# Graph layer on one core: the message stage takes y rows from an on-chip table and sums equal sources before the second linear map

## The reference, cut to what matters

```
ys = xs @ w1_s * inv;  yv = einsum('nud,uv->nvd', xv, w1_v) * inv      # y, 256 per node
w  = radial network of edge_attr_8 (three linear maps)                 # wA, wB, wC, wD per edge
es, ev = ys[dst], yv[dst];  sh0, sh1 = edge_attr_4 split
m0a = wA * es * sh0;              m0b = wD * sum_d(ev * sh1) / sqrt(3)
m1a = wB * es * sh1 (per d);      m1b = wC * ev * sh0
ns = segment_sum([m0a, m0b], src);  nv = segment_sum([m1a, m1b], src)  # and the degree
out = ns * dn @ w2_s ...,  nv * dn @ w2_v ...                          # second linear map
```

## Time and profile before

| | us |
|---|---|
| runs, median of three (lowest to highest) | 8281.1 (8236.3 to 8301.24) |
| span of the profiled execution, first to last instruction | 7531.3 |
| median less that span | 749.8 |
| message stage in the profile, 2960 to 7237 | 4277, so 5.14 for each of 832 steps |
| attention stage, 170 to 2600 | 2430 |
| node stage, 2604 to 2955 | 351, so 3.58 for each of 98 blocks |
| last stage | 294 |

### The profile page before, as it was taken

One profiled execution on the slowest core, in us unless ns is written; L12 is line 12 of the kernel. 1 busy time (PEld: TensorE's weight loads), 2 busy tenths in 40 slices (PEclk: granted clock), 3 DMA queues, 4 the chain that ended last, 5 costly groups with the idle time before them and its releaser, 6 DMA issues.

```text
span 7531.3 us, 218435 instructions
## 1 busy us (share of the span) xinstructions
PE 6552.1 (87%) x36547; PEld 4301.1 (57%) x36548; DVE 5437.6 (72%) x20339; ACT 4022.4 (53%) x12733; POOL 5759.5 (76%) x4888
## 2 busy tenths in 40 slices
PE   6999999999999988888888888888888888888876
PEld 5666666666666555555555555555555555555544
DVE  3788888888888798666666666666666666666668
ACT  2455555555555455555555555555555555555532
POOL 3677777777777655888888888888888888888878
PEclk8899999999999999999999999999999999999999
DMA  5788888888888766777777777777777777777789
GB/s 178 200 224 223 224 225 224 222 224 226 224 223 223 207 221 192 136 136 135 136 135 135 136 136 136 136 135 136 135 135 137 136 136 135 136 136 135 136 227 299
DMA packets 1268411, 1312.20 MB, mean 174 GB/s; under 512 B 232303, under 2 KB 1153040, under 8 KB 1268272
## 3 DMA queue, kind: packets, MB, share of 16 engines
q0 software_dynamic: 368112, 577.39, 45.5%
q1 hardware_dynamic: 900258, 734.36, 33.8%
HBM read 723.28 MB, written 587.78 MB: 174 GB/s over the span
## 4 chain that ended last, share of the span: by engine, by line
PE 38%; issue 23%; POOL 19%; DMA 8%; DVE 7%; POOLq 2%; ACT 2%; DVEq 1%; ACTq 0%; SPq 0%
POOL part L571 13%; PE PS L845 12%; PE PS L837 12%; DMA part<-arena,c_idx 8%; POOL d_out L562 5%; PE PS L866 3%; PE PS L862 2%; PE PS L959 2%; PE PS L952 1%; PE PS L878 1%; ACT arena L724 1%; DVE arena L1310 1%; PE PS L871 1%; PE PS L789 1%; DVE arena L1298 1%
## 5 line engine op out<-in xcount | busy, mean ns | idle before, releaser
L571 POOL DMA_INDIRECT part<-arena,c_idx x1664 | 2671.4, 1605 | 515.8 <-issue 457.7
L522 POOL DMA_INDIRECT arena<-h_tab,sidx x1664 | 1773.8, 1066 | 634.9 <-issue 385.7
L1279 DVE SCALAR_TENSOR_TENSOR arena<-PS,c_src,lower_eq 128x128 f32<-128x128 f32 x1664 | 517.6, 348 | 1385.1 <-PE PS L964 1385.1
L717 ACT COPY arena<-PS 128x514 f32<-128x514 f32 x832 | 489.7, 589 | 1823.5 <-DMA part<-arena,c_idx 1823.3
L952 PE MATMUL PS<-ident,arena 128*128 128x128 f32 x3328 | 545.1, 286 | 679.7 <-ACT arena L724 666.5
L921 PEld LDWEIGHTS PS<-ident,arena 128*128 128x128 f32 x6656 | 739.8, 141 | 626.9 <-issue 582.7
L562 POOL DMA_INDIRECT d_out<-y_tab,c_row x832 | 829.2, 997 | 266.6 <-issue 252.6
L921 PE MATMUL PS<-ident,arena 128*128 128x128 f32 x6656 | 977.0, 280 | 61.5 <-issue 43.0
L710 ACT COPY arena<-PS 128x512 f32<-128x512 f32 x1664 | 991.7, 603 | 6.8 <-PE PS L921 6.7
L1157 DVE TENSOR_TENSOR big<-big,PS 128x260 f32 x1664 | 703.9, 423 | 396.2 <-PE PS L845 336.1
L845 PE MATMUL PS<-arena 128*128 128x260 f32 x3328 | 961.4, 412 | 3.5 <-DVE big L1157 2.2
(11 more groups left out here) (192 smaller groups left out, 11545.7 us busy)
## 6 DMA issues: line engine op xcount, KB each, us to landing
w_tab<-arena SPq DMA_DIRECT2D x416, 520.0 KB
arena<-w_tab SPq DMA_DIRECT2D x1664, 130.0 KB
part<-zeros SPq DMA_DIRECT2D x1664, 32.1 KB
arena<-part SPq DMA_DIRECT2D x392, 128.5 KB, 3.4
arena<-h_tab,sidx POOLq DMA_INDIRECT x1664
ot_tab<-arena SPq DMA_DIRECT2D x416, 64.0 KB
arena<-ot_tab SPq DMA_DIRECT2D x416, 64.0 KB
part<-arena,c_idx POOLq DMA_INDIRECT x1664
```

The costliest lines, as they stand in the source:

```text
L522: pool.indirect_dma_start(hg[:, s, k, :], None, h_tab, bass.IndirectOffsetOnAxis(ap=sidx[:, s, k:k + 1], axis=0)).then_inc(s_hg[s], 16)
L571: pool.indirect_dma_start(part[q], bass.IndirectOffsetOnAxis(ap=c_idx[:, s, k:k + 1], axis=0), o_cmb[:, q, :], None, compute_op=ALU.add).t ...
```

## The change

1. The node stage splits each y into three bfloat16 parts that add up to it, kept on chip in `y3` (ACT writes the high and the middle part, DVE makes the two remainders). y_tab, its stores and the gathers are gone; both tiles of every pair get y rows by PE, as the sum of three bfloat16 products for each tile. ot_tab now holds all four one-hot matrices of a group. Its bfloat16 form is used as it is.
2. `same` is now the plain equality of sources, without `lower_eq` and counts. The messages are multiplied by it where they were transposed (`combine`, L915): that product is the transposed sum over equal sources, so the product after the second map and one evacuation are gone.
3. Four small PE products for each pair (`count`) give the degree and a number that tells which edge of a source is its first; ACT copies them to `c_num`, DVE compares for the row numbers.
4. The numbers of blocks for y are loaded eight at a time, once in four steps, on PE.
5. Buffers move: the attention stage's lie beside `acc` in `big`, `o_cmb` has four slots, `midT` one instead of two.

```
 node stage, ACT and DVE
-                    a.copy(acc[:, ds(b - 2, 1), 0:D]..., maps[:, :, 0, :]).then_inc(s_bout, 1)
+                    a.copy(y3[:, ds(b - 2, 1), 0, :]..., maps[:, :, 0, :])
+                if there(b - 2):
+                    wait(act, s_br, b - 1)
+                    a.copy(y3[:, ds(b - 2, 1), 1, :].rearrange("p o d -> p (o d)"), b_r[:, s % 2, :]).then_inc(s_bmid, 1)
+                if there(b - 3):
+                    wait(dve, s_bmid, b - 2)
+                    v.tensor_tensor(y3[:, ds(b - 3, 1), 2, :]..., b_r[:, (s + 1) % 2, :], y3[:, ds(b - 3, 1), 1, :]..., ALU.subtract).then_inc(s_blo, 1)
+                if there(b - 2):
+                    wait(dve, s_bout, b - 1)
+                    v.tensor_tensor(b_r[:, s % 2, :]..., maps[:, :, 0, :], y3[:, ds(b - 2, 1), 0, :]..., ALU.subtract).then_inc(s_br, 1)
 message stage, POOL
-                n = (s + 6) % TURN
-                if n % 2 and there(u + 6):
-                    wait_apart(pool, s_crow, u + 7)
-                    wait_apart(pool, s_cmid, u + 3)
-                    for k in range(PAIR):
-                        pool.indirect_dma_start(c_y[:, n // 2, k, :], None, y_tab, ...)
-                    wait_apart(pool, s_cix, 3 * (u + 1))
+                    wait_apart(pool, s_cix, 2 * (u + 1))
-                                                o_cmb[:, q, :], None, compute_op=ALU.add).then_inc(s_add[q], 16)
+                                                o_cmb[:, s, k, :], None, compute_op=ALU.add).then_inc(s_add[q], 16)
 message stage, PE
-                def transpose(k):
+                def combine(k):
                     wait(pe, s_cmid, u)
                     wait(pe, s_cmT, PAIR * (u - 2) + k + 1)
                     for j in range(4):
-                        last = nc.tensor.transpose(PS[:, T_BANK[k], j * P:(j + 1) * P], mid[...], ident[:, :])
+                        last = mm(PS[:, T_BANK[k], j * P:(j + 1) * P], mid[...], same[:, m, k, :], start=True, stop=True)
                     last.then_inc(s_cmt, 1)
+                def count():
+                    wait(pe, s_cnum, u - 1)
+                    for k in range(PAIR):
+                        eq = same[:, m, k, :].bitcast(BF16)[:, 1::2]
+                        mm(counts[:, k, 0:1], eq, valid[:, ds((u - 1) * PAIR + k, 1)], start=True, stop=True)
+                        last = mm(counts[:, k, 1:2], eq, rank_b[:, :], start=True, stop=True)
+                    last.then_inc(s_ccnt, 1)
-                if n % 2 == 0 and there(u + 1):
-                    b = numbers(pe, block_row, (u + 1) * PAIR, PAIR, NB)
+                if s == 0 and there(u + 1):
+                    turn_blocks[0] = numbers(pe, block_row, (u + 1) * PAIR, (TURN if there(u + 4) else TURN - 1) * PAIR, NB)
-                    wait(pe, s_cotf, u + 3)
                     wait(pe, s_cmid, u)
+                    b = turn_blocks[0][s * PAIR:(s + 1) * PAIR]
                     for k in range(PAIR):
-                        last = mm(PS[:, 0, k * D:(k + 1) * D], c_otf[:, n // 2, k, :], acc[...], start=True, stop=True)
-                    last.then_inc(s_cy, 2)
+                        for i in (2, 1, 0):
+                            last = mm(PS[:, Y_BANK[n % 2], k * D:(k + 1) * D], c_ot[:, n // 2, n % 2 * PAIR + k, :],
+                                      y3[:, ds(b[k], 1), i, :]..., start=(i == 2), stop=(i == 0))
+                    last.then_inc(s_cy, 1)
-                if there(u - 3):
-                    wait(pe, s_csame, PAIR * (u - 2))
-                    wait(pe, s_cosb, u - 2)
-                    wait(pe, s_ccmb, u - 3)
-                    for k in range(PAIR):
-                        last = mm(PS[:, 6 + k, 0:OR], same[:, o, k, :], o_sb[:, o % 2, k, :], start=True, stop=True)
-                    last.then_inc(s_cc, 1)
 message stage, ACT (the whole of a step now)
+                if there(u - 2):
+                    wait(act, s_ccnt, u - 1)
+                    a.copy(c_num[:, (s + 2) % TURN, :, :], counts).then_inc(s_cnum, 1)
+                if there(u - 3):
+                    wait(act, s_co, u - 2)
+                    for k in range(PAIR):
+                        wait(act, s_add[q + k], 8 * (u - 3) - 8 * (o % 2) - 16 if there(u - 7) else 0)
+                    a.copy(o_cmb[:, o, :, 0:D]..., PS[:, O_BANK, :]...)
+                    a.copy(o_cmb[:, o, :, D], c_num[:, o, :, 0]).then_inc(s_ccmb, 1)
                 if there(u - 2):
                     wait(act, s_coT, u - 1)
                     a.copy(oT_sb[:, :, :], PS[:, OT_BANK, :]...).then_inc(s_coTsb, 1)
                 if there(u - 1):
                     transposed(0)
                     transposed(1)
```

More of the change, by code:

```diff
@@ new lines, in bass_gat_equivariant_kernel, with cut_of @@
+        big = sb("big", [P, BIG])
+        ACC = BIG - NB * HW
+        TABLES = 2 * EW + 2 * T + 4 * NC * P
+        assert ACC * NB >= 0 and TABLES <= NB * HW and (3 * D // 2 - HW) * NB <= ACC
+        acc = big[:, ACC:].rearrange("p (b d) -> p b d", d=HW)
+        y3 = big[:, :].bitcast(BF16).rearrange("p (b i d) -> p b i d", i=3, d=D)
+        tables = big[:, ACC:]
+        ARENA = 10400
+        arena = sb("arena", [P, ARENA])
+        used = {}
+        def cut_of(name, where, limit, n, at=None):
+            at = used.get(name, 0) if at is None else at
+            used[name] = at + n
+            assert used[name] <= limit, (name, used[name], limit)
+            return where[:, at:at + n]
@@ new lines, in bass_gat_equivariant_kernel @@
+        bounds = cut_a(2)
+        cnt = cut_a(8)
+        two = cut_a(33)
+        b128 = cut_a(NC)
+        tile_col = cut_a(NC)
+        wcol = cut_a(NC).bitcast(I32)
+        skw = cut(2 * D, True).rearrange("p (k n) -> p k n", k=2)
+        brow = cut(D)[0:1, :]
+        wm = cut(4 * P).rearrange("p (k m u) -> p k m u", k=2, m=2)
+        ones = cut(P)
+        pself = cut(NB * H).rearrange("p (b h) -> p b h", h=H)
+        rden = cut(NB * H).rearrange("p (b h) -> p b h", h=H)
+        B_KEPT = used["arena"]
@@ L718, in step_c @@
-                if there(u + 1):
-                    wait_apart(act, s_cix, 3 * (u - 2))
-                    a.copy(c_src[:, n, :], srcF[:, ds((u + 1) * PAIR, PAIR)]).then_inc(s_csl, 1)
+                    a.copy(midT[:, k, :, :], PS[:, T_BANK[k], :].rearrange("p (c e) -> p c e", c=4)).then_inc(s_cmT, 1)
+                if there(u - 2):
+                    wait(act, s_ccnt, u - 1)
+                    wait(act, s_cix, 2 * (u - 5))
+                    a.copy(c_num[:, (s + 2) % TURN, :, :], counts).then_inc(s_cnum, 1)
@@ L937, in step_c @@
                 if there(u - 1):
-                    transpose(0)
-                if n % 2 == 0 and there(u + 1):
-                    wait(pe, s_cotf, u + 3)
+                    combine(0)
+                if there(u + 1):
+                    if n % 2 == 0:
+                        wait(pe, s_cin[n], landed(u + 1, n, 2))
                     wait(pe, s_cmid, u)
+                    b = turn_blocks[0][s * PAIR:(s + 1) * PAIR]
                     for k in range(PAIR):
-                        last = mm(PS[:, 0, k * D:(k + 1) * D], c_otf[:, n // 2, k, :],
-                                  acc[:, ds(b[k], 1), 0:D].rearrange("p o d -> p (o d)"), start=True, stop=True)
-                    last.then_inc(s_cy, 2)
+                        for i in (2, 1, 0):
+                            last = mm(PS[:, Y_BANK[n % 2], k * D:(k + 1) * D], c_ot[:, n // 2, n % 2 * PAIR + k, :],
+                                      y3[:, ds(b[k], 1), i, :].rearrange("p o d -> p (o d)"),
+                                      start=(i == 2), stop=(i == 0))
+                    last.then_inc(s_cy, 1)
@@ L946, in step_c @@
                 if there(u - 1):
-                    transpose(1)
+                    combine(1)
+                    count()
                 if there(u - 2):
                     wait(pe, s_coTsb, u - 1)
-                    wait(pe, s_cosb, u - 2)
+                    wait(pe, s_ccmb, u - 2)
                     for j in range(4):
-                        last = nc.tensor.transpose(PS[:, 5, j * P:(j + 1) * P], oT_sb[:, j, :], ident[:, :])
+                        last = nc.tensor.transpose(PS[:, O_BANK, j * P:(j + 1) * P], oT_sb[:, j, :], ident[:, :])
@@ L966, in _ @@
-            steps(pe, NU, 1, 3, step_c)
+                    wait(pe, s_csame, u + 1)
+                    mm(PS[:, SR_BANK, 0:PAIR * P], ones_b[:, :], c_parts[:, n // 2, n % 2 * PAIR * P:(n % 2 + 1) * PAIR * P],
+                       start=True, stop=True).then_inc(s_csr, 1)
+            steps(pe, NU, 1, 2, step_c)
             pe.wait_ge(s_ccmb, NU)
@@ L1255, in step_b @@
                     wait(dve, s_brstd, b)
-                    wait(dve, s_bst[m], landed(b - 5, m, 2) if there(b - 5) else 0)
+                    wait(dve, s_bst[m], landed(b - 5, m) if there(b - 5) else 0)
                     normalized(b_x1[:, m, 0:MUL], b_v[:, m, 0:MUL], m).then_inc(s_bx1, 1)
```

(6 more changed lines are left out.)

352 lines of the change are left out of this document (152 added, 200 removed).

## The result

| | us | runs |
|---|---|---|
| before, median (lowest to highest) | 8258.7 (8225.79 to 8301.24) | 4 |
| changed kernel | 8973.53 (8937.48 to 8992.4) | 4 |
| ratio, 95% interval | 1.0868 (1.0823 to 1.0913) | |

The forecast was 8305 us with a range of 8020 to 8560 us. The time lies 413 us above the range.

What follows compares the result with a forecast made beforehand. POOL's queue was taken as the bound, PE close behind. Changed, PE's 4.54 + 0.55 us made a 5.10 us step; span 7531.3 - 34 + 65 - 7 = 7555, plus 749.8 around it: 8305 us, range 8020 to 8560.

Steps and rivals of the forecast that it cites:

- POOL bounds the kernel before: Message stage: POOL's scatters and gathers set the 5.11 us step; without gathers its queue falls to 3.81 us.
- PE's step: Message stage: PE's own work sums to 4.54 us a step, before the wait for block numbers.
- Combining: PE, message stage: 16 instructions of combining products at the transposes' 0.117 us each, 1.87 us a step.
- The switches: PE, message stage: four more changes of product form, 0 to 0.4 us a step, taken as 0.1.
- Rival (b): PE, message stage: weight loads of 128-column float32 products aren't hidden; at 0.14 us a load 8613 us; chance 0.15.
- Rival (c): PE, message stage: combining products cost four times the transposes seen, 0.47 us each; 9861 us; chance 0.02.
- The loop through ACT: Message stage: with one midT the second map waits for ACT's copy; a 4.45 us floor hidden under PE's 4.54.
- Node stage: Two added DVE subtractions of 256 columns, 0.66 us a block: 65 us more, range 25 to 95.
- Attention stage: PE's work there is unchanged and ot_tab's stores double: 0, at most 20 us more.
- The block numbers: PE, message stage: loading eight takes 3.16 us; PE stands 2.0 to 2.2 us once in four steps, taken as 0.55 a step.
- a rival on the fast side: Message stage: numbers load in 0.33 us, starting early, and switches cost nothing; 4.75 us a step, 8004 us; chance 0.27.
- 749.8 us around the span: Outside the traced span: 749.8 us of unexplained time, left unchanged and added to the 7555 us span.

Runs made afterwards that it cites:

- between_transposes: As load_behind, but load of two numbers ahead of the counts, and eight transposes instead of the combining products (sum over equal sources left out): 6479.78 us, third chip.
- load_behind: Changed kernel, with PE loading two block numbers every step, behind both sets of combining products and the counts: 7055.9 us, 0.9384 of the kernel before, second chip.
- shifted_numbers: Changed kernel with the row of block numbers shifted six places, so loads of eight start at multiples of 32 bytes: 7655.85 us, 1.0185 of the kernel before, second chip.
- two_numbers: Changed kernel, with PE loading two block numbers in every step at the same place, instead of eight once in four: 7988.9 us, 0.9675 of the kernel before.

## Why the prediction was wrong

Right, by the prediction's own steps:
- **POOL bounds the kernel before, and its queue falls to 3.81 us a step.** Met at 3.78 us once PE was made short enough (between_transposes).
- **PE's step.** 4.54 us forecast; 4.48 in the undisturbed step shown, 4.45 in the mean without numbers. Combining 1.87 us forecast, 1.89 measured (5003.53 to 5005.42 in load_behind); y 0.65 forecast, 0.66 measured (5006.23 to 5006.89). The switches were misread, with little effect: rows 6 leave 0.62 less 0.43, 0.19 us, for one change of form, not 0.1. Rival (b) falls: a weight load lasts 0.192 us and still hides. Rival (c) falls: by it the step would be 6.97 us. The Trainium skill, "TensorE: Matmul & The Clock Gate", Terms, says that the transpose mode is four times as fast for FP32. Measured against a float32 product, it is twice as fast here (0.109 against 2 x 0.112 us), and the measurement decides.
- **The loop through ACT.** Forecast as a floor at 4.45 that costs nothing; the second map waited for ACT 5 times in the stage, 1.9 us in all (the changed kernel on the third chip). That the step without numbers is 4.45 us too is no proof of the floor.
- **Node stage.** 65 us more forecast; L1242 starts 98 times from 3296.5 to 3703.8 us, 4.20 us a block, where it was 3.54 (L1249, 3229.6 to 3573.5, in the same chip's run of before): 0.66 us, 64 us. Its rows: 

```profile
L1242 DVE TENSOR_TENSOR arena<-arena,PS x98: 405/408/422, 3296.5 to 3703.8; 128x256 f32<-128x256 f32 x98
```

- **Attention stage** 0 to 20 us: 2 us where the clock is the same; on the slower chip 66 us, whose cause stays open.

Wrong:
- **"The block numbers", the load's duration.** I took 0.78 us for eight numbers from a row with two. The change from two to eight was the one size in this term that the trace didn't show, and the rows at hand (0.78 us for two, 0.33 for four) contradicted each other, which I read as "quick here, slow there" and kept as a rival on the fast side alone. It should have been bounded upwards too: eight times a number's price at two, 0.39, is 3.1 us. Nor was 0.78 us a fixed price for two: in the kernel before this load took 0.53 to 0.93 us, for reasons that no run shows. The load of eight took 2.08 us, so PE stood 3.6 us once in four steps instead of 2.0 to 2.2, which is 0.90 us a step instead of 0.55.
- **The clock.** No term of the sum had it, though the new idle time of PE, over 2 us once in four steps, was in the forecast itself. It costs 0.62 us a step. The trace before gave some ground for leaving it out: the message stage had 1.00 with PE waiting for ACT 380 times, up to 1.9 us. But the forecast gap lay beyond that, and no upper bound was put on its price. With a gap as long as forecast (shifted_numbers) the clock cost 0.14 us a step.
- Together: the forecast was 4.54 + 0.55 + 0, the measured step is 4.45 + 0.90 + 0.62, 5.96 us before rounding. 0.35 us for the load and 0.62 for the clock were missing, 0.09 for PE's own work was too much: 0.86 us a step, 719 us in the stage. That shifted_numbers comes to 5.12 us, so near the forecast's 5.10, is partly luck: 4.45 + 0.53 + 0.14.
- **749.8 us around the span.** They don't exist. In each later run the time is 1.7 us more than the span (8280.38 and 8278.7 us for the kernel before). The profile before was most likely taken on a quicker chip than the timed runs. This did the forecast little harm: the message stage before differs by 0.14 us a step between the two profiles (5.12 and 5.26), some 120 us, where the miss is 719.

## What to carry to other kernels

A load of numbers into registers is executed by the engine's sequencer, and the engine pays for that part of it and of its register steps that is longer than the work queued in front of it. Batching such loads lengthens the one gap, and the gap can cost the clock behind it as well. So keep them short and frequent, and put them behind a long run of issued work: the first turned a ratio of 1.087 into 0.9675 here, both together gave 0.938 (on another chip). When two rows of the trace price the same operation differently, the difference is a cause that isn't yet named; vary it (place, count) before taking one of the two, and carry the range both ways.

## What the runs showed of the hardware

- A load of block numbers by PE's sequencer took 1.00 and 2.08 us for 4 and 8 numbers that start two behind a multiple of four, and 0.33 and 0.59 us for 4 and 8 that start at one. Two numbers took 0.54 us at either place (two_numbers), but up to 0.9 us in other kernels. VectorE's sequencer does the same (four numbers: 0.35 us, and 1.02 us with the shift). Each number costs 0.29 us more in register steps. The lengths look like one read for four numbers where the load starts at a multiple of four, and one for each number where it doesn't, even if a whole group of four lies inside; that is a reading of the lengths, not shown.
- PE's granted clock fell to half within or behind idle times of 3.6 us in each cycle of four steps, of 2.8 us in 205 of 208 cycles, and of 2.1 us in 70 of 208. It stayed at 1.00 with idle times of 1.36 us once in two steps (four numbers), and in the kernel before with waits of up to 1.9 us. In the changed kernel it was back within 5.8 us behind the gap.
- In a run of them, a float32 product of 128 columns with new weights costs 0.224 us, two instructions 0.112 us apart, weight loads of 0.192 us hidden; a float32 transpose costs 0.109 us. The first instruction of a run adds some 0.1 us.
- Two chips ended the attention stage at about 2570 to 2594 us (2644 with the shifted numbers) and one at 3217 to 3298, with clocks of 0.98 to 0.99 and 0.86 to 0.88.
